# A hybrid layer in fp32 on one core: scales moved from GpSimd to ScalarE, residual sums moved between engines, and new instruction orders

## The chip, the cores and the metric

The kernel runs on one core of a Trainium2 chip. The metric is the device time of one launch in microseconds (us). The engines are TensorE (PE in the profile, with its weight loads as PEld), VectorE (DVE), ScalarE (ACT), GpSimd (POOL) and SyncE (SP).

## What is computed

The input is `x` of 8 batches, 512 tokens and 128 channels, in fp32. Four sub-layers are added to it in turn:

```python
x = x + attn_a(layernorm(x))      # q = n Wq ; (q n^T) n, no softmax
x = x + ffn(layernorm(x))         # f1
x = x + attn_b(layernorm(x))      # RWKV: time mixing, then channel mixing
x = x + ffn(layernorm(x))         # f2, the same weights as f1

# ffn: only expert 0 counts
h = relu(tgt @ w1[0] + b1[0]);  y = tgt + h @ w2[0] + b2[0]
return (y - mean(y)) * rsqrt(var(y) + 1e-5) * gamma + beta

# attn_b
k, v, r = xk @ Wk.T, xv @ Wv.T, xr @ Wr.T       # xk, xv, xr mix a token with the one before
x = x + (sigmoid(r) * wkv(k, v)) @ Wo.T         # wkv: a scan over tokens
kk = square(relu(xk2 @ ffn_Wk.T))
return x + sigmoid(xr2 @ ffn_Wr.T) * (kk @ ffn_Wv.T)
```

Each layer norm and each output of an ffn needs a scale `(var + eps)^-0.5` for each token.

## The kernel before

Each batch is a tile `R[b]` of 128 partitions and 4 rows of 128 tokens (`J = 4`). The residual stream lives in `R[b]` from the first load to the store. The work is cut into small helper functions, one for each batch and step (`attn_gram(b, bank)`, `hidden_up(b, f, n, bank)`, `z_stats(b, f, bank)`), and each engine calls its helpers in an order that is written out by hand, one long list for each engine. So an engine does exactly the next item of its list, and where this item waits on a semaphore, all behind it wait too. Batches are at different sub-layers at the same time, and the eight PSUM banks are dealt out by the numbers in the lists.

The steps that matter here:

- The layer norms: DVE takes the statistics (`row_stats`, `mean_var`), POOL makes the scale in `shift` (an addition of eps), `power` (a power of -0.5) and `bias`, and ACT applies it in `normed`. The first tile is done in two halves (`first_stats`, `first_mean_var`, `first_shift`, `first_power`, `first_normed`, the last one on DVE).
- The attention: PE makes the Gram matrix of the normed tile (`attn_gram`, L1089), the transposes (`transposed`, L1076), the projection (`attn_proj`, L1097) and the product (`attn_apply`, L1104), with an ACT copy out of PSUM after each of the first three. DVE adds the result to `R` (`attn_out`, L535).
- The ffn: transposes of the normed tile, `ffn_evacuate`, four `hidden_up` (L1117) with a `relu` on ACT after each (L907), four `ffn_down` (L1126) that add up in one bank. The sum in this bank begins with the ffn's own input (`y = tgt + ...`). For the batches in `STARTED` DVE writes it there (`ffn_start`, L712). For the others PE does, by four transposes (its own `ffn_start`, L1237). PE's other matmuls of 512 columns are `cmix_up` (L1188) and the three products of the time mixing (L1159, L1164, L1169).
- The ffn's output: `z_stats` and `mean_var` on DVE, then `z_shift` (L341) and `power` (L346) on POOL make `f_zn_rs`, and DVE's `ffn_scaled` (L566) multiplies by it and by gamma. The result is added to `R` in one of two ways: by a DMA with accumulation that POOL starts (`ffn_sum`, L382), or for the batches in `ADDED` by DVE (`ffn_add`, L573). The channel mixing's result has the same two ways: `cmix_sum` (L390, a DMA from POOL) and `cmix_out` (L703, on DVE).
- The last tile is done in two halves: `last_down`, `last_stats`, `last_mean_var`, `last_shift`, `last_power`, `last_scaled`, `last_out`, and a store for each half.

ACT loads one table at its start, `natural_log_exp_and_others`, and no other.

## Time and profile before

| | |
|---|---|
| median of 3 runs | 262.93 us (262.4 to 263.28) |
| the profiled execution: its own time | 264.55 us |
| the profiled execution: span from the first to the last instruction | 262.8 us |
| mean granted TensorE clock | 0.994 |
| PE busy | 253.0 us (96%) |
| DVE busy | 232.7 us (89%) |
| ACT busy | 227.4 us (87%) |
| POOL busy | 153.1 us (58%) |
| DMA | 16.53 MB |

Times in the rows are in microseconds from the start of the span. "Busy" is the union of an engine's instructions. The profiled execution took 1.62 us longer than the median of the runs. PE's instructions are pipelined: a row of one matmul shows more than the distance to the next one.

### The profile page before, as it was taken

The page shows a single profiled execution, that of the slowest core. Times are in us where ns is not written, and L with a number is a line of the kernel's source. Part 1 is how long each engine was busy: PE and PEld are TensorE (multiplying, and loading weights), DVE is VectorE, ACT ScalarE, POOL GpSimd, SP SyncE. Part 2 cuts the span into 40 slices and gives each one's busy share as a digit, 9 for nine tenths or more (in the row PEclk, how much of TensorE's full clock was granted, in tenths as well). Part 3 has the DMA queues.
Part 4 walks back from the last instruction along what each step waited for, and adds up shares of the span by engine and source line. Part 5 has one row for each costly group of instructions (what it writes and reads, how often), then busy time and mean ns, then how long its engine had stood idle before and what let it go on. Part 6 is the DMA issues. An engine that isn't in the chain of part 4 may idle for free.

```text
span 262.8 us, 5291 instructions
## 1 busy us (share of the span) xinstructions
PE 253.0 (96%) x1508; PEld 189.6 (72%) x1508; DVE 232.7 (89%) x762; ACT 227.4 (87%) x439; POOL 153.1 (58%) x290
## 2 busy tenths in 40 slices
PE   7999999999999999999999999999999999999991
PEld 6877686778777686667677767757874977777771
DVE  4598699999999999999999999999999987816384
ACT  1589899988988999899999999999999999993640
POOL 4558788832984774657927166964817158353522
PEclk9999999999999999999999999999999999999997
DMA  7922202402024220222403142063222526450332
GB/s 204 300 90 41 41 2 41 80 0 42 1 44 80 40 40 4 40 41 42 81 1 60 22 80 42 1 115 69 50 49 49 110 46 108 94 114 12 64 96 80
DMA packets 16908, 16.53 MB, mean 63 GB/s; under 512 B 1392, under 2 KB 11504, under 8 KB 16880
## 3 DMA queue, kind: packets, MB, share of 16 engines
q0 software_dynamic: 5616, 10.23, 22.9%
q1 hardware_dynamic: 10848, 5.84, 8.0%
q8 instruction: 12, 0.20, 0.3%
q10 hardware_dynamic: 416, 0.14, 0.2%
q14 instruction: 16, 0.13, 0.2%
HBM read 3.87 MB, written 2.10 MB: 23 GB/s over the span
## 4 chain that ended last, share of the span: by engine, by line
PE 84%; ACT 4%; POOL 4%; issue 3%; DVE 3%; DMA 1%; DVEq 0%; ACTq 0%; POOLq 0%
PE bank L1117 19%; PE bank L1126 19%; PE bank L1188 10%; PE bank L1194 8%; PE bank L1076 7%; PE bank L1089 3%; PE bank L1104 3%; PE bank L1169 3%; PE bank L1164 3%; PE bank L1205 2%; PE bank L1175 2%; PE bank L1159 2%; PE bank L1237 1%; DMA R<-in_hidden 1%; ACT f_h L907 1%
## 5 line engine op out<-in xcount | busy, mean ns | idle before, releaser
L1126 PEld LDWEIGHTS bank<-W,f_h 128*128 128x128 f32 x480 | 59.0, 192 | 12.0 <-issue 11.0
L1117 PE MATMUL bank<-f_yT,W 128*128 128x512 f32 x128 | 63.3, 595 | 0.0
L1126 PE MATMUL bank<-W,f_h 128*128 128x128 f32 x480 | 60.8, 275 | 0.0
L1194 PEld LDWEIGHTS bank<-FWv,KK 128*128 128x128 f32 x256 | 30.9, 192 | 3.4 <-issue 2.6
L1194 PE MATMUL bank<-FWv,KK 128*128 128x128 f32 x256 | 32.2, 276 | 0.0
L1188 PE MATMUL bank<-XK,FWk 128*128 128x512 f32 x64 | 30.5, 596 | 0.8 <-ACT KK L964 0.6
L1117 PEld LDWEIGHTS bank<-f_yT,W 128*128 128x128 f32 x128 | 21.2, 191 | 12.4 <-issue 7.8
L840 ACT ACTIVATE f_y<-R,f_yn_nb,f_yn_rs 128x128 f32<-128x128 f32 x64 | 26.3, 484 | 3.3 <-POOL f_yn_nb L350 3.1
L907 ACT ACTIVATE f_h<-bank,B1C 128x512 f32<-128x512 f32 x36 | 24.3, 686 | 0.2 <-PE bank L1126 0.2
L907 ACT ACTIVATE f_h<-bank,B 128x512 f32<-128x512 f32 x28 | 18.6, 681 | 6.0 <-PE bank L1126 3.3
L293 POOL TENSOR_TENSOR f_yn_ve<-f_yn_mv,K_EPS 128x4 f32<-128x4 f32 x16 | 7.3, 457 | 25.1 <-DVE f_yn_mv L529 25.1
L374 POOL DMA_DIRECT2D R<-BETA x16 | 16.8, 1068 | 6.1 <-ACT f_y L840 5.4
L1188 PEld LDWEIGHTS bank<-XK,FWk 128*128 128x128 f32 x64 | 11.4, 190 | 12.3 <-issue 8.0
L968 ACT ACTIVATE KK<-KK 128x512 f32<-128x512 f32 x32 | 19.6, 633 | 0.2
L341 POOL TENSOR_TENSOR f_zn_ve<-f_zn_mv,K_EPS 128x4 f32<-128x4 f32 x15 | 8.7, 579 | 18.9 <-DVE f_zn_mv L529 18.9
L566 DVE SCALAR_TENSOR_TENSOR f_zg<-bank,f_zn_rs,GAMMA 128x128 f32<-128x128 f32 x56 | 15.6, 339 | 3.5 <-issue 3.3
L964 ACT ACTIVATE KK<-bank 128x512 f32<-128x512 f32 x32 | 18.3, 586 | 0.4 <-PE bank L1188 0.3
L446 DVE BATCH_NORM_STATS2 f_zn_stats<-bank 128x6 f32<-128x128 f32 x60 | 13.2, 280 | 5.6 <-PE bank L1126 5.5
L346 POOL TENSOR_TENSOR f_yn_rs<-f_yn_ve,K_RSQRT 128x4 f32<-128x4 f32 x16 | 16.6, 1037 | 0.0
L346 POOL TENSOR_TENSOR f_zn_rs<-f_zn_ve,K_RSQRT 128x4 f32<-128x4 f32 x15 | 16.1, 1071 | 0.7
L382 POOL DMA_DIRECT2D R<-f_zg x11 | 10.0, 908 | 11.0 <-DVE f_zg L566 10.1
L840 ACT ACTIVATE N<-R,tmix_nb,tmix_rs 128x128 f32<-128x128 f32 x32 | 13.1, 484 | 1.1 <-POOL tmix_nb L350 0.9
(160 smaller groups left out, 637.2 us busy)
## 6 DMA issues: line engine op xcount, KB each, us to landing
R<-BETA POOLq DMA_DIRECT2D x16, 256.0 KB, 3.4
R<-f_zg POOLq DMA_DIRECT2D x11, 256.0 KB, 3.4
R<-N POOLq DMA_DIRECT2D x8, 256.0 KB, 3.7
R<-in_hidden SPq DMA_DIRECT2D x7, 256.0 KB, 5.6
out_x<-R SPq DMA_DIRECT2D x7, 256.0 KB, 2.3
R<-G POOLq DMA_DIRECT2D x4, 256.0 KB, 3.5
W<-in_w SPq DMA_DIRECT2D x2, 256.0 KB, 5.1
BETA<-in_beta SPq DMA_DIRECT2D x1, 256.0 KB, 5.2
```

The lines of the kernel that those rows point to most:

```text
L346: pool.tensor_tensor(n.rs[b % 2][:], n.ve[b % 2][:], K_RSQRT[:], ALU.pow).then_inc(n.scale.sem(b), 1)
L374: pool.dma_start(R[b][:], BETA[:], accum_op=ALU.add).then_inc(*f.xb.step(b))
L566: last = v.scalar_tensor_tensor(zg[:, j, :], z[:, j, :], f.znorm.rs[b % 2][:, j:j + 1], GAMMA[:], ALU.mult, ALU.mult)
L840: done = a.activation(dst[:, j, :], src[:, j, :], ACT.Identity, scale=n.rs[b % 2][:, j:j + 1], bias=n.nb[b % 2][:, j:j + 1])
L907: a.activation(at(f.h, b)[:, n, :], banks[bank][:], ACT.Relu, bias=bias[:, n:n + 1]).then_inc(f.h_ready[n], 1)
L964: a.activation(at(KK, b)[:, n, :], banks[bank][:], ACT.Relu).then_inc(square[n].sem(b), 1)
L968: a.activation(at(KK, b)[:, n, :], at(KK, b)[:, n, :], ACT.Square).then_inc(square[n].sem(b), 1)
L1076: last = t_.matmul(banks[bank][:, j * P:(j + 1) * P], src[:, j, :], IDENT[:], start=(j == 0), stop=(j == J - 1), is_transpose=True, skip_g ...
L1117: t_.matmul(banks[bank][:], W1[:, n * P:(n + 1) * P], at(f.yT, b)[:], start=True, stop=True).then_inc(f.h_psum[n], 1)
L1126: last = t_.matmul(banks[bank][:, j * C:(j + 1) * C], at(f.h, b)[:, n, j * P:(j + 1) * P], W2[:, n, :], start=False, stop=(n == H - 1), sk ...
L1188: t_.matmul(banks[bank][:], FWk[:, n * P:(n + 1) * P], at(XK2, b)[:], start=True, stop=True).then_inc(kk_psum[n], 1)
L1194: last = t_.matmul(banks[bank][:, j * C:(j + 1) * C], at(KK, b)[:, n, j * P:(j + 1) * P], FWv[:, n, :], start=(n == 0 and j == 0), stop=(n ...
```

## The change

Four things change.

1. ACT makes some scales that POOL made before, as `exp(-0.5 * ln(var + eps))` with two activations from the table that is already loaded: for the two halves of the first tile (`first_log`, `first_root`), for all outputs of both ffns (`z_log`, `z_root`) and for the two halves of the last one (`last_log`, `last_root`). That is 19 pairs (2, 15 and 2), 38 activations. `z_shift`, `first_shift`, `last_shift` and the powers that follow them are gone from POOL's list.
2. `ADDED` shrinks from (0, 4), (5, 6, 7), (0, 1, 6, 7) to (0,), (7,), (7,). Three `ffn_add` (f1: 4; f2: 5, 6) and three `cmix_out` (0, 1, 6) leave DVE, and six DMAs with accumulation join POOL's list. `ffn_add` has no call left and is removed.
3. `STARTED` of f2 grows from (5, 6, 7) to (4, 5, 6, 7): one more sum is begun in PSUM by DVE, and one group of four PE transposes goes away. This makes eight such sums.
4. All lists are in a new order, with new bank numbers. Nothing else changes in what is computed.

```diff
-ADDED = {"f1": (0, 4), "f2": (5, 6, 7), "x3": (0, 1, 6, 7)}
+ADDED = {"f1": (0,), "f2": (7,), "x3": (7,)}
-STARTED = {"f1": (0, 1, 2, 3), "f2": (5, 6, 7)}
+STARTED = {"f1": (0, 1, 2, 3), "f2": (4, 5, 6, 7)}
...
-            def ffn_add(b, f, tile):
-
-                dve.wait_ge(f.zg_ready, b + 1)
-                dve.wait_ge(*f.xb.ready(b))
-                v.tensor_tensor(R[b][:], at(tile, b)[:], R[b][:], ALU.add).then_inc(*f.out.step(b))
...
+            def log_rows(n, rows, wait, b, done):
+
+                act.wait_ge(*wait)
+                if b >= 2:
+                    act.wait_ge(f2.zg_ready, b - 1)
+                c = slice(rows[0], rows[-1] + 1)
+                a.activation(n.ve[b % 2][:, c], n.mv[b % 2][:, c, 1], ACT.Ln, bias=K_EPS[:, 0:1]).then_inc(done, 1)
+
+            def root_rows(n, rows, wait, b, done):
+
+                act.wait_ge(*wait)
+                c = slice(rows[0], rows[-1] + 1)
+                a.activation(n.rs[b % 2][:, c], n.ve[b % 2][:, c], ACT.Exp, scale=-0.5).then_inc(done, 1)
...
+            def z_log(b, f):
+                n = f.znorm
+                act.wait_ge(const_ready, 8)
+                act.wait_ge(n.mv_ready, b + 1)
+                if b >= 2:
+                    if b - 2 in f.split:
+                        act.wait_ge(*f.out.ready(b - 2))
+                    else:
+                        act.wait_ge(f.zg_ready, b - 1)
+                a.activation(n.ve[b % 2][:], n.mv[b % 2][:, :, 1], ACT.Ln, bias=K_EPS[:, 0:1]).then_inc(n.scale.sem(b), 1)
+
+            def z_root(b, n):
+
+                act.wait_ge(*n.scale.done(b, "ve"))
+                a.activation(n.rs[b % 2][:], n.ve[b % 2][:], ACT.Exp, scale=-0.5).then_inc(n.scale.sem(b), 1)
...
-            gram_evacuate(0, 0); attn_evacuate(0, 1); proj_evacuate(0, 0); attn_normed(1); attn_normed(2)
+            first_log(0); first_root(0); first_log(1); first_root(1); gram_evacuate(0, 1); attn_evacuate(0, 0)
...
-            attn_gram(0, 0); attn_transpose(0, 1); attn_proj(0, 0); bias_rows(); attn_apply(0, 0)
+            attn_transpose(0, 0); attn_gram(0, 1); attn_proj(0, 1); attn_apply(0, 1); attn_transpose(1, 0)
```

The first place is the start of PE's list. The rows before, from the warm-up matmuls (L1213) on:

```order
1 L1213 MATMUL bank<-WROW 128x128 x10
2 L1089 MATMUL bank<-XN 128x128 x4
3 L1076 MATMUL bank<-IDENT,XN 128x128 x4
4 L1097 MATMUL bank<-GRAM,Wq 128x128
5 L1220 MATMUL bank<-DIAG,MEAN 128x128
6 L1221 MATMUL bank<-VEC,MEAN 128x1
7 L1104 MATMUL bank<-PROJ,XNT 128x128 x4
8 L1076 MATMUL bank<-IDENT,XN 128x128 x4
```

And the same place after the change (L1114 are transposes, L1127 the Gram matrix, L1135 the projection, L1142 the product, L1258 the bias rows):

```order
1 L1251 MATMUL bank<-WROW 128x128 x10
2 L1114 MATMUL bank<-IDENT,XN 128x128 x4
3 L1127 MATMUL bank<-XN 128x128 x4
4 L1135 MATMUL bank<-GRAM,Wq 128x128
5 L1142 MATMUL bank<-PROJ,XNT 128x128 x4
6 L1114 MATMUL bank<-IDENT,XN 128x128 x4
7 L1127 MATMUL bank<-XN 128x128 x4
8 L1114 MATMUL bank<-IDENT,XN 128x128 x4
9 L1135 MATMUL bank<-GRAM,Wq 128x128
10 L1127 MATMUL bank<-XN 128x128 x4
11 L1258 MATMUL bank<-DIAG,MEAN 128x128
```

The first tile's transposes now stand ahead of its Gram matrix, and the bias rows, which stood between the projection and the product, stand behind the third Gram matrix. On ACT, further down, the transposes' copy `attn_evacuate(3)` and `attn_normed(3)` also stand earlier, so that PE has the transposes and the Gram matrix of the fourth tile ahead of the first `hidden_up`.

The second place is in the middle of ACT's list, around the exponents of the time mixing's third tile. Before (L927 to L940 are the four passes over the exponents, L885 and L896 copies out of PSUM, L964 a relu):

```order
88 L927 ACTIVATE EB<-EA 128x1024
89 L896 ACTIVATE f_yT<-bank,B2C 128x512
90 L885 ACTIVATE PROJ<-bank 128x128
91 L932 ACTIVATE EA<-EA 128x2x512
92 L936 ACTIVATE EB<-EB 128x1024
93 L940 ACTIVATE EA<-EA 128x2x512
94 L964 ACTIVATE KK<-bank 128x512
```

After (the same passes are L915, L920, L924 and L928; L1012 is `z_log`, L1017 `z_root`):

```order
101 L915 ACTIVATE EB<-EA 128x1024
102 L861 ACTIVATE XNT<-bank 128x512
103 L884 ACTIVATE f_yT<-bank,B2C 128x512
104 L924 ACTIVATE EB<-EB 128x1024
105 L873 ACTIVATE PROJ<-bank 128x128
106 L1012 ACTIVATE f_zn_ve<-f_zn_mv,K_EPS 128x4
107 L920 ACTIVATE EA<-EA 128x2x512
108 L934 ACTIVATE G<-bank 128x512
109 L928 ACTIVATE EA<-EA 128x2x512
110 L1017 ACTIVATE f_zn_rs<-f_zn_ve 128x4
```

The scale of an ffn output has joined the line, its logarithm and its exponential apart, with three other activations between them.

The third place is in DVE's list, at the ffn output of the fifth tile of f1. Before (L566 scales it, L573 adds it to `R`; L648 is a sum of the time mixing):

```order
130 L566 SCALAR_TENSOR_TENSOR f_zg<-bank,f_zn_rs,GAMMA 128x128 x4
131 L624 TENSOR_TENSOR EA<-EA,bank 128x512
132 L643 TENSOR_TENSOR AB<-AB,EB 128x2x512
133 L579 TENSOR_TENSOR DX<-XA 128x512
134 L573 TENSOR_TENSOR R<-f_zg,R 128x512
135 L648 TENSOR_TENSOR EA<-AB,EA 128x1024
```

After (the scaling is L560, and the sum of the time mixing L636):

```order
128 L560 SCALAR_TENSOR_TENSOR f_zg<-bank,f_zn_rs,GAMMA 128x128 x4
129 L523 BN_AGGR f_yn_mv<-f_yn_stats 128x2 x4
130 L607 TENSOR_TENSOR EV<-EB,bank 128x512
131 L612 TENSOR_TENSOR EA<-EA,bank 128x512
132 L677 SCALAR_TENSOR_TENSOR DC<-DC,VEC,XC 128x512
133 L567 TENSOR_TENSOR DX<-XA 128x512
```

The addition is gone from DVE; POOL starts a DMA for it instead. In the same way `cmix_out(0)` and `cmix_out(1)` are gone further down.

## Rows read from the trace of the kernel before

**Rows 1.** The page's busy line: us (share of the span) xinstructions.

```profile
PE 253.0 (96%) x1508; PEld 189.6 (72%) x1508; DVE 232.7 (89%) x762; ACT 227.4 (87%) x439; POOL 153.1 (58%) x290
```

**Rows 2.** PE's groups by shape: names, shapes xcount | busy us, mean ns.

```profile
L1117 PE MATMUL bank<-f_yT,W 128*128 128x512 f32 x128 | 63.3, 595 | 0.0
...
L1188 PE MATMUL bank<-XK,FWk 128*128 128x512 f32 x64 | 30.5, 596 | 0.8 <-ACT KK L964 0.6 <-ACT f_h L907 0.2
...
L1159 PE MATMUL bank<-XK,Wk 128*128 128x512 f32 x16 | 8.3, 600 | 0.0
...
L1237 PE MATMUL bank<-IDENT,f_yT 128*128 128x128 f32 x36 | 5.5, 276 | 0.0
```

**Rows 3.** The chain of work that ended last: start us, us, what.

```profile
18.95 3.44 PE bank L1117 x8
23.28 2.68 PE bank L1126 x24
```

**Rows 4.** The timeline of the first 20 us: start us, us, engine, instructions [idle before].

```profile
1.46 4.64 PE L1213 MATMUL bank<-WROW 128*128 128x128 f32 x20 [1.46 <-DVE WROW L723]
...
4.56 0.25 DVE L457 BATCH_NORM_AGGREGATE attn_mv<-attn_stats 128x2 f32<-128x6 f32 x2
...
6.40 0.60 DVE L471 TENSOR_SCALAR XN<-R,attn_mv,attn_rs 128x128 f32<-128x128 f32 x2 [0.33 <-POOL attn_rs L308]
...
7.15 2.04 PE L1089 MATMUL bank<-XN 128*128 128x128 f32 x8 [1.05 <-DVE XN L471]
...
8.99 1.06 PE L1076 MATMUL bank<-IDENT,XN 128*128 128x128 f32 x4
9.23 0.28 ACT L879 ACTIVATE GRAM<-bank 128x128 f32<-128x128 f32 x1 [6.17 <-PE bank L1089]
...
9.84 0.63 PE L1097 MATMUL bank<-GRAM,Wq 128*128 128x128 f32 x2
...
10.58 0.27 ACT L885 ACTIVATE PROJ<-bank 128x128 f32<-128x128 f32 x1
...
10.73 3.18 ACT L840 ACTIVATE XN<-R,attn_nb,attn_rs 128x128 f32<-128x128 f32 x8
...
15.87 1.65 ACT L840 ACTIVATE f_y<-R,f_yn_nb,f_yn_rs 128x128 f32<-128x128 f32 x4
...
18.79 3.60 PE L1117 MATMUL bank<-f_yT,W 128*128 128x512 f32 x8
```

**Rows 5.** Stretches: us, busy us (xcount) of PE, PEld, DVE, ACT, POOL, clock, DMA.

```profile
7.00:20.00 13.00, 12.44 (x77) 10.93 (x78) 9.95 (x62) 9.54 (x27) 7.10 (x17) 1.00 0.70 192
...
80.00:220.00 140.00, 138.66 (x804) 100.18 (x804) 138.51 (x396) 136.53 (x251) 82.26 (x140) 1.00 0.29 51
...
220.00:240.00 20.00, 20.00 (x134) 16.03 (x133) 11.81 (x40) 18.49 (x37) 8.88 (x16) 1.00 0.48 93
```

**Rows 6.** ACT's smallest activations, whole span.

```profile
L993 ACT ACTIVATE WDEC<-WEXP 128x1 f32<-128x1 f32 x1 | 0.2, 203 | 0.0
L991 ACT ACTIVATE WEXP<-VEC 128x1 f32<-128x1 f32 x1 | 0.2, 194 | 0.0
```

**Rows 7.** DVE's additions to R that leave it, between 40 and 200 us.

```profile
L703 DVE TENSOR_TENSOR R<-G,R 128x512 f32<-128x512 f32 x2 | 1.4, 675 | 0.0
L573 DVE TENSOR_TENSOR R<-f_zg,R 128x512 f32<-128x512 f32 x1 | 0.7, 676 | 0.0
```

**Rows 8.** POOL's shifts of the ffn outputs, between 80 and 220 us.

```profile
L341 POOL TENSOR_TENSOR f_zn_ve<-f_zn_mv,K_EPS 128x4 f32<-128x4 f32 x7 | 5.1, 727 | 5.9 <-DVE f_zn_mv L529 5.9
```

**Rows 9.** The DMA issues: count, KB each, median us to landing.

```profile
R<-G POOLq DMA_DIRECT2D x4, 256.0 KB, 3.5
```

**Rows 10.** The timeline of the end.

```profile
255.32 1.95 PE L1146 MATMUL bank<-W,f_h 128*128 128x128 f32 x16
...
256.42 0.49 DVE L451 BATCH_NORM_STATS2 f_zn_stats<-bank 128x6 f32<-128x128 f32 x2 [0.29 <-PE bank L1146]
...
258.71 1.18 DVE L497 SCALAR_TENSOR_TENSOR R<-f_zg,f_zn_rs,R 128x128 f32<-128x128 f32 x4
```

More of the change, by code:

```diff
@@ L826, in _ @@
[L826 to L828 removed]
+            warm_tile(); first_stats(0); first_mean_var(0); first_stats(1); first_mean_var(1); first_normed(0)
+            first_normed(1); attn_stats(1); mean_var(1, na); attn_stats(2); mean_var(2, na); attn_stats(3)
@@ new lines, in _ @@
+            ffn_out(0, f1); tmix_stats(0); mean_var(0, nt); attn_out(3, 2); decay_along_tokens(); ffn_stats(3, f1)
+            attn_stats(7); mean_var(3, f1.norm); mean_var(7, na); ffn_start(2, f1, 4, (f1.h_ready[3], 2))
+            z_stats(1, f1, 0); mean_var(1, f1.znorm); tmix_change(0); mix_k(0); ffn_scaled(1, f1, 0); mix_v(0)
+            mix_r(0); running_max(0, 1); differences(0, 1); ffn_start(3, f1, 5); attn_out(4, 2); tmix_stats(1)
+            mean_var(1, nt); ffn_stats(4, f1); mean_var(4, f1.norm); z_stats(2, f1, 4); new_values(0, 6)
@@ new lines, in _ @@
+            denominator_sum(0); numerator_sum(0); first_values(0, 6); weighted(0); mean_var(2, f1.znorm)
+            with_current(0); tmix_change(1); gate_sum(0); mix_k(1); ffn_scaled(2, f1, 4); gate_log(0, 1)
+            running_max(1, 3); gated(0); mix_v(1); differences(1, 3); attn_out(5, 6); tmix_out(0, 0); ffn_stats(5, f1)
+            mix_r(1); mean_var(5, f1.norm); up_bias(7); tmix_stats(2); first_values(1, 1); mean_var(2, nt)
+            cmix_stats(0); new_values(1, 1); mean_var(0, ncm); z_stats(3, f1, 5); denominator_sum(1); numerator_sum(1)
@@ new lines, in _ @@
+            attn_out(6, 6); weighted(1); mean_var(3, f1.znorm); ffn_stats(6, f1); with_current(1)
+            mean_var(6, f1.norm); tmix_change(2); gate_sum(1); mix_k(2); ffn_scaled(3, f1, 5); gate_log(1, 0)
+            running_max(2, 1); mix_v(2); gated(1); mix_r(2); differences(2, 1); z_stats(4, f1, 3); tmix_stats(3)
+            mean_var(4, f1.znorm); mean_var(3, nt); cmix_change(0); tmix_out(1, 6); cmix_k(0); cmix_stats(1)
+            attn_out(7, 6); mean_var(1, ncm); ffn_stats(7, f1); ffn_scaled(4, f1, 3); mean_var(7, f1.norm)
@@ new lines, in _ @@
+            z_stats(6, f1, 7); weighted(3); tmix_change(4); with_current(3); ffn_stats(0, f2); gate_sum(3)
+            mean_var(0, f2.norm); mix_k(4); mix_v(4); gate_log(3, 1); ffn_scaled(5, f1, 5); running_max(4, 2)
+            gated(3); cgate_log(1, 6); differences(4, 2); cmix_change(2); mean_var(6, f1.znorm); tmix_stats(5)
+            cmix_gated(1, 4); cmix_k(2); mean_var(5, nt); tmix_out(3, 5); mix_r(4); ffn_scaled(6, f1, 7)
+            cmix_stats(3); denominator_sum(4); cmix_r(2); new_values(4, 3); mean_var(3, ncm); first_values(4, 3)
@@ new lines, in _ @@
+            mean_var(2, f2.norm); first_values(5, 4); weighted(5); tmix_change(6); with_current(5); mix_k(6)
+            gate_sum(5); cmix_change(4); cmix_k(4); tmix_stats(7); gate_log(5, 1); mean_var(7, nt); running_max(6, 3)
+            gated(5); cgate_log(3, 4); mix_v(6); cmix_r(4); differences(6, 3); cmix_gated(3, 0); mix_r(6)
+            z_stats(0, f2, 5); mean_var(0, f2.znorm); tmix_out(5, 0); cmix_stats(5); mean_var(5, ncm)
+            ffn_scaled(0, f2, 5); tmix_change(7); ffn_stats(3, f2); mix_k(7); new_values(6, 0); mean_var(3, f2.norm)
@@ L831, in _ @@
+            last_mean_var(1); last_scaled(1, 1); last_out(0); last_out(1)
         @block.scalar
```

487 lines of the change are left out of this document (233 added, 254 removed).

## The prediction

> **What bounds the kernel now.** I read the page's busy line first [rows 1]: PE is busy for 96% of the span, DVE for 89%, ACT for 87%, POOL for 58%. A busy PE is not yet a PE at its peak, since the ends of its instructions are modelled. So I turned to the pace. In the chain of work, 24 matmuls of 128 columns take 2.68 us and 8 of 512 columns 3.44 us [rows 3], that is 0.112 and 0.43 us each. The groups by shape give the counts [rows 2]: 128 and 64 of 512 columns, and three groups of 16 like the one shown, 240 in all. The page has 1508 matmuls [rows 1], of which 20 are the warm-up [rows 4], so 1248 are narrow. The work is 240 x 0.43 + 1248 x 0.112 = 242.6 us. PE does it between 7.15 us, when the first Gram matrix starts, and 257.27 us, when the last matmul ends (255.32 + 1.95) [rows 4, 10]. That is 250.1 us, so 7.5 us are lost in between. Of these, 3.3 us fall before 20 us: 77 matmuls start there, the last three of them wide, worth 9.6 us, in the 12.85 us from 7.15 on [rows 5]. Only 4.2 us are left for the other 237 us. PE is the bound nearly everywhere, and a gain can come from four places: less work on PE, an earlier start, a shorter end, and the 4.2 us.
>
> The stretches say what stands right behind PE [rows 5]. Between 80 and 220 us DVE is idle for 1.49 of 140 us and ACT for 3.47. Both are nearly full, and an engine that gets more work there can take over as the bound.
>
> **The change part by part.** *One sum more begun in PSUM by DVE.* PE has 36 transposes for it in nine groups of four [rows 2] and loses one group: 4 x 0.112 = 0.45 us off the bound. DVE writes 512 columns more, 0.68 us by an addition of this size [rows 7]; by its tile it lies between 220 and 240 us, where DVE was idle for 8.2 us [rows 5]. Without this cover it would cost 0.68.
>
> *The first tile's scale on ACT.* The statistics of its second half are done at 4.81 us (4.56 + 0.25), the normed half begins at 6.40 after a wait for POOL, and ends at 7.00 [rows 4]. ACT needs two activations. The nearest rows are two of one column, 0.19 and 0.20 us [rows 6]; a bound from above is the copy of 128 columns, 0.28 us [rows 4]. I take 0.2 each, 0.4 for a pair, since four columns are nearer to one than to 128. With it the second half can be normed from about 5.4 to 6.05 us (DVE has the first half from 4.85). PE's warm-up ends at 6.10 [rows 4], so PE loses its 1.05 us of idle time there and starts real work at about 6.05, 1.1 us earlier.
>
> It doesn't keep all of it. The transposes now go first, 0.85 us (four at 0.21, from 1.06 us with the modelled end), so that the Gram matrix starts at 6.9 and its copy at 8.95 + 0.05, against 9.23. Then the projection needn't wait for the transposes until 9.84: it starts at 9.3 and its copy at 10.0, against 10.58. So `attn_normed(1)` and the two behind it are some 0.6 us earlier (from 10.73, 3.18 us for two tiles) [rows 4], and end at about 13.3. From there I add up ACT's list in its new order, with durations from the rows: a Gram copy 0.27, two copies of 512 columns 1.06 in the old run's pace (0.53 each), a projection copy 0.27, `attn_normed(3)` 1.6, a Gram copy 0.27, the ffn's first normed tile 1.65. The sum is 5.1, so this tile ends at 18.4, against 17.52. In the old run the first `hidden_up` starts 1.27 us behind that end [rows 4]; now it would be at 19.7 with this distance, and at 19.3 if ACT's instructions overlap as in the old run (eight activations of a normed tile take 3.18 us, though each takes 0.48 by itself). I take 19.3: half a microsecond later than the old 18.79. But by then PE has done the transposes and the Gram matrix of the fourth tile as well, 4 + 8 = 12 matmuls or 1.34 us, which stood behind it before. Net: 1.34 - 0.5 = 0.85 us. The bounds are 0.45 (start at 19.7) and 1.3 (no delay at all).
>
> *The end.* `last_scaled(0)` moves into the wait between the statistics and their mean. The rest of the chain is DVE's own: from 256.42 to 259.89 (258.71 + 1.18) it does 3.3 us of work, and POOL's scale isn't what it waits for [rows 10]. ACT's faster scale gives nothing here, the new order perhaps 0.15 us; bounds 0 and 0.3.
>
> *The ffn outputs' scales on ACT.* In the stretch from 80 to 220 us POOL made seven of them [rows 8]. Seven pairs at 0.4 are 2.8 us, less than ACT's 3.47 us of idle time, so I cost them at nothing; the cover is thin. With 0.28 for an activation it would be 3.9 us, 0.45 over. Behind each logarithm stand copies and relus that PE waits for, and it waits itself for DVE's `mean_var`.
>
> The Trainium skill says in "ScalarE: Activation LUTs", "Rules for kernel authors", that a tight latency budget should count about 0.3 us for each ACTIVATE and 0.83 ns for each element. By this rule a pair would cost about 0.61 us, seven pairs 4.3 us, ACT would be 0.8 us over, and the sum would give 262.3 us. The rows of one column show 0.19 and 0.20 us, so the trace does not agree; it has no row of this form with four columns.
>
> *Six sums to POOL's DMAs.* Three of them leave DVE between 80 and 200 us, 3 x 0.68 = 2.0 us [rows 7], more than DVE's idle time there. The result lands 3.5 us after the issue [rows 9], 2.8 later than by DVE. The tile is next read by `tmix_stats` or `ffn_stats`, and the lists hold other batches' work ahead of those. POOL gives up 19 scales for six DMAs, and is idle for 57.7 of 140 us [rows 5] before. I cost it at nothing, with the relief of DVE as a possible gain inside the 4.2 us.
>
> *New orders in the middle.* I can't add up 237 us of four lists from rows. The loss there was 4.2 us, and this bounds the gain. I take no change: DVE has 2.0 us less, ACT 2.8 us more, and both were near full.
>
> The sum is 0.45 + 0.85 + 0.15 = 1.45 us. The profiled execution goes from 264.55 to 263.1; its own time is 1.62 us above the median of the runs shown, and I take the same step off the median: 262.93 - 1.45 = 261.5 us.
>
> **The rivals.** *A, the forecast:* 261.5 us, by itself between 260.6 and 262.3. Chance 0.47.
>
> *B, the middle tightens.* DVE's three additions are gone, its queue runs ahead, and half of the 4.2 us goes: 261.5 - 2.1 = 259.4 us. For it: DVE was idle for only 1% between 80 and 220 us. Against: ACT gets the work instead. A second source would be the pace at the start. The eight matmuls at 7.15 take 2.04 us, 0.21 apart where the granted clock's column has 1.00 [rows 4, 5]; that is the pace of 1.2 GHz, half of that of [rows 3], after PE had been idle for 1.05 us. Without this idle time the change to the fast pace may come sooner, which would shorten the transposes and the Gram matrix by up to 1.2 us. Chance 0.17.
>
> *C, ACT becomes the bound (slower).* The place is `z_log` in ACT's list. POOL waited 5.9 us for DVE's `mean_var` ahead of these seven scales [rows 8], at no cost, since nothing urgent stood behind it. On ACT the relus for PE stand behind. If ACT waited as long, it would be 2.8 + 5.9 - 3.5 = 5.2 us over, and the time 266.7. With 60% of the wait, 3.5 us, it is 2.8 over: 264.3 us, my figure for this case. It is slower by more than the measurement can tell from 2.2 us over on, that is from 2.9 us of waits. For it: DVE is as full as ACT and its delay would pass on directly. Against: in the second place of the order `z_log` stands five activations behind the exponents' first pass, while DVE has the statistics and mean right behind the differences that this pass waits for; a list of this kind may keep the waits short. Chance 0.20.
>
> *D, the start gives nothing.* PE starts earlier but the chain of copies, `attn_normed(3)` above all, holds the first `hidden_up` back until 20.1 us, and the 12 matmuls done ahead only make up for it. Then 0.45 + 0.15 are left, 262.3 us, and with a microsecond lost on a new wait 263.3. Chance 0.16.
>
> **How the numbers follow.** About 0.3% of 262.93 us, 0.79 us, is what a measurement of this kernel can tell from no change: the bounds are 262.14 and 263.72. Faster: nine tenths of A and all of B, 0.42 + 0.17, and a little of D, 0.61 in all. Slower: C and a rest of D, 0.20. Same: 0.19. The likeliest is A, 261.5. The range takes in B's 259.4 with its own spread down to 259.0 and C's 264.3 at the other end; below 259.0 and above 264.3 I leave 0.1 each.
>
> **What would show it.** In the new profile: the first transpose at about 6.05 us and no idle time behind the warm-up; the first `hidden_up` at 19.3; 32 transposes of the group that had 36; activations of four columns of about 0.2 us; ACT's idle time between 80 and 220 us near 0.7, and no wait of ACT for `f_zn_mv` above a microsecond in sum; the work of PE 0.45 us less and its loss after 20 us still about 4.2. The prediction is wrong if that loss is above 6 (C) or below 2.5 (B), or if the logarithms wait for DVE.

## The result, and the profile after

The changed kernel takes 259.39 us (median of 4 runs, 259.09 to 259.62), and the kernel before on the same chip 262.95 us (262.4 to 263.28). The ratio is 0.9845 with a 95% interval of 0.9803 to 0.9887. The gain is 3.6 us, where 1.45 was predicted. The new time lies inside the range of 259.0 to 264.3 us, on rival B's figure of 259.4.

Executions of the kernel before come near 262.9, 264.3 and 265.8 us, and the one shown ahead of the prediction took 264.55. So I profiled the same kernel again (`b_again`, profiled execution 263.11 us, span 261.3), and compare with that where a microsecond matters. The profiled execution of the changed kernel took 259.21 us, with a span of 257.4.

From the page of the changed kernel and its groups by shape: the busy line, the shares of the chain that ended last (PE had 84% of it before), the group of wide matmuls for `FWk`, and the DMA issues of the sums (KB each, median us to landing).

```profile
PE 249.5 (97%) x1504; PEld 187.8 (73%) x1504; DVE 231.2 (90%) x757; ACT 231.9 (90%) x477; POOL 133.2 (52%) x258
...
PE 94%; DVE 2%; DMA 1%; ACT 1%; POOL 1%; issue 0%; DVEq 0%; POOLq 0%; ACTq 0%
...
L1226 PE MATMUL bank<-XK,FWk 128*128 128x512 f32 x64 | 32.0, 597 | 0.0
...
R<-G POOLq DMA_DIRECT2D x7, 256.0 KB, 3.4
...
R<-f_zg POOLq DMA_DIRECT2D x14, 256.0 KB, 4.0
```

PE has four matmuls fewer, which are the four transposes. In [rows 2] the `FWk` group had 0.8 us of idle time ahead of its members. Now it has none.

The stretches of the changed kernel, with the columns of [rows 5]:

```profile
7.00:20.00 13.00, 11.84 (x86) 10.02 (x86) 11.61 (x70) 10.87 (x30) 7.77 (x22) 1.00 0.69 192
...
80.00:220.00 140.00, 139.97 (x831) 102.88 (x831) 136.06 (x387) 138.66 (x268) 72.76 (x128) 1.00 0.30 53
100.00:200.00 100.00, 100.00 (x588) 72.92 (x587) 99.59 (x279) 99.46 (x192) 50.83 (x90) 1.00 0.29 51
...
220.00:240.00 20.00, 20.00 (x120) 14.83 (x119) 14.52 (x57) 15.79 (x36) 5.54 (x11) 1.00 0.45 87
```

And the same hundred microseconds of the kernel before, in its second profile:

```profile
100.00:200.00 100.00, 98.70 (x567) 70.53 (x566) 99.61 (x273) 97.80 (x179) 60.39 (x100) 1.00 0.26 46
```

PE's column is the one to read. Between 80 and 220 us it goes from 138.66 to 139.97 of 140 us, and between 100 and 200 us it is now full. ACT goes from 136.53 to 138.66, which leaves it 1.34 us of idle time. The view of PE's waits names neither ACT nor another engine after the first 20 us. In the kernel before it named ACT three times, for 0.6, 0.4 and 0.2 us, and VectorE never. These are the first two, from the second profile (us in all, times, longest):

```profile
PE bank L1188 <- ACT KK L964: 0.6, 1, 0.6
PE bank L1076 <- ACT f_h L907: 0.4, 1, 0.4
```

Each of the two stands behind an activation of ACT that had waited in its turn for a product of POOL (`tmix_nb` and `cmix_nb`, the biases of two norms). So the old kernel's losses run through ACT and POOL as well as through VectorE.

Modelled ends hide part of a wait, so I counted the loss as the prediction did: from the start of each matmul to that of the next, less its own 0.112 or 0.43 us [rows 3]. Counted to the start of the last matmul, the 4.2 us of the prediction are 4.0.

| | first profile before | second profile before | after |
|---|---|---|---|
| first real matmul starts | 7.15 | 7.03 | 5.88 |
| lost from there to 20 us | 3.38 | 2.04 | 2.66 |
| lost from 20 to 100 us | 0.80 | 0.79 | 0.42 |
| lost from 100 to 200 us | 2.71 | 2.70 | 0.71 |
| lost from 200 us to the last matmul | 0.51 | 0.51 | 0.23 |
| span | 262.8 | 261.3 | 257.4 |

The two profiles of the kernel before differ at the head alone. After 20 us they lose the same time.

Of 3.9 us of span, 2.0 come from the middle, 0.45 from the transposes, some 0.5 from the start (1.15 earlier, 0.6 more lost), 0.4 and 0.3 from the stretches on both sides of the middle. What is left, some 0.25 us, is the end. From the last tile's first statistics to the last sum's end the new timeline has 254.41 - 251.32 = 3.1 us, where [rows 10] has 3.5; behind it comes the last store, which ends 2.9 to 3.3 us later in five profiles of the changed kernel and its small edits.

The timeline of the changed kernel's head, and of its end:

```profile
1.46 4.63 PE L1251 MATMUL bank<-WROW 128*128 128x128 f32 x20 [1.46 <-DVE WROW L711]
...
4.35 0.29 ACT L982 ACTIVATE attn_ve<-attn_mv,K_EPS 128x2 f32<-128x2 f32 x1 [1.29 <-DVE attn_mv L451]
...
4.68 0.20 ACT L988 ACTIVATE attn_rs<-attn_ve 128x2 f32<-128x2 f32 x1
...
5.88 0.98 PE L1114 MATMUL bank<-IDENT,XN 128*128 128x128 f32 x4
...
6.70 1.06 PE L1127 MATMUL bank<-XN 128*128 128x128 f32 x8
...
9.17 3.19 ACT L828 ACTIVATE XN<-R,attn_nb,attn_rs 128x128 f32<-128x128 f32 x8 [0.18 <-POOL attn_nb L350]
...
18.15 3.60 PE L1155 MATMUL bank<-f_yT,W 128*128 128x512 f32 x8
...
251.32 0.49 DVE L445 BATCH_NORM_STATS2 f_zn_stats<-bank 128x6 f32<-128x128 f32 x2 [2.60 <-PE bank L1184]
...
253.28 1.13 DVE L491 SCALAR_TENSOR_TENSOR R<-f_zg,f_zn_rs,R 128x128 f32<-128x128 f32 x4
```

PE no longer waits behind the warm-up. The Gram matrix's eight matmuls take 1.06 us from 6.70 on, where [rows 4] has 2.04 from 7.15 on. `attn_normed(1)` begins at 9.17 instead of 10.73.

ACT's new instructions, by their lines (duration ns least/median/greatest, first and last start; and below each, what it waited for in us, times):

```profile
L1012 ACT ACTIVATE f_zn_ve<-f_zn_mv,K_EPS x15: 280/294/315, 27.3 to 247.0; 128x4 f32<-128x4 f32 x15
...
  DVE f_zn_mv L523: 1.7, 2
...
L1017 ACT ACTIVATE f_zn_rs<-f_zn_ve x15: 191/198/217, 27.6 to 247.3; 128x4 f32<-128x4 f32 x15
...
  DVE f_zg L560: 1.0, 1
```

A pair is 0.49 us, not 0.4. ACT waits 1.7 us for `f_zn_mv` in the whole span, in two places, and not at all between 80 and 220 us, where POOL had waited 5.9 [rows 8].

### The profile page after: what moved, and what is told of

Its sections match the earlier page's. It is cut to its first block, busy times and chain, and to the rows that moved or that the text cites. A ratio compares the mean times of both kernels' runs of the same rounds, so it can differ in the third digit from the quotient of the medians.

```text
span 257.4 us, 5284 instructions
## 1 busy us (share of the span) xinstructions
PE 249.5 (97%) x1504; PEld 187.8 (73%) x1504; DVE 231.2 (90%) x757; ACT 231.9 (90%) x477; POOL 133.2 (52%) x258
## 4 chain that ended last, share of the span: by engine, by line
PE 94%; DVE 2%; DMA 1%; ACT 1%; POOL 1%; issue 0%; DVEq 0%; POOLq 0%; ACTq 0%
PE bank L1155 21%; PE bank L1164 21%; PE bank L1232 11%; PE bank L1226 11%; PE bank L1114 7%; PE bank L1213 3%; PE bank L1243 3%; PE bank L1197 3%; PE bank L1207 3%; PE bank L1202 3%; PE bank L1142 3%; PE bank L1127 2%; PE bank L1275 1%; DMA R<-in_hidden 1%; PE bank L1175 1%; PE bank L1135 1%
## 5 line engine op out<-in xcount | busy, mean ns | idle before, releaser
L1164 PEld LDWEIGHTS bank<-W,f_h 128*128 128x128 f32 x480 | 58.2, 192 | 8.7 <-issue 8.6
L1155 PE MATMUL bank<-f_yT,W 128*128 128x512 f32 x128 | 61.2, 593 | 0.0
L1226 PE MATMUL bank<-XK,FWk 128*128 128x512 f32 x64 | 32.0, 597 | 0.0
L895 ACT ACTIVATE f_h<-bank,B 128x512 f32<-128x512 f32 x32 | 21.2, 681 | 5.5 <-PE bank L1155 4.2
L390 POOL DMA_DIRECT2D R<-G x7 | 6.3, 897 | 36.4 <-DVE G L686 36.4
L895 ACT ACTIVATE f_h<-bank,B1C 128x512 f32<-128x512 f32 x32 | 21.4, 682 | 0.1
L382 POOL DMA_DIRECT2D R<-f_zg x14 | 14.1, 1006 | 13.4 <-DVE f_zg L560 11.2
L346 POOL TENSOR_TENSOR f_yn_rs<-f_yn_ve,K_RSQRT 128x4 f32<-128x4 f32 x16 | 19.3, 1206 | 0.0
L560 DVE SCALAR_TENSOR_TENSOR f_zg<-bank,f_zn_rs,GAMMA 128x128 f32<-128x128 f32 x56 | 15.6, 338 | 3.2 <-issue 2.2
L374 POOL DMA_DIRECT2D R<-BETA x16 | 15.7, 1037 | 4.6 <-ACT f_y L828 4.0
L1226 PEld LDWEIGHTS bank<-XK,FWk 128*128 128x128 f32 x64 | 10.7, 190 | 8.2 <-issue 4.4
L440 DVE BATCH_NORM_STATS2 f_yn_stats<-R 128x6 f32<-128x128 f32 x64 | 13.7, 275 | 0.1
```

The source lines that it names most:

```text
L346: pool.tensor_tensor(n.rs[b % 2][:], n.ve[b % 2][:], K_RSQRT[:], ALU.pow).then_inc(n.scale.sem(b), 1)
L374: pool.dma_start(R[b][:], BETA[:], accum_op=ALU.add).then_inc(*f.xb.step(b))
L440: last = v.bn_stats(n.stats[b % 2][:, j, :], src[:, j, :])
L895: a.activation(at(f.h, b)[:, n, :], banks[bank][:], ACT.Relu, bias=bias[:, n:n + 1]).then_inc(f.h_ready[n], 1)
L1155: t_.matmul(banks[bank][:], W1[:, n * P:(n + 1) * P], at(f.yT, b)[:], start=True, stop=True).then_inc(f.h_psum[n], 1)
L1164: last = t_.matmul(banks[bank][:, j * C:(j + 1) * C], at(f.h, b)[:, n, j * P:(j + 1) * P], W2[:, n, :], start=False, stop=(n == H - 1), sk ...
```

## The experiments

Each ran beside the kernel before on the same chip. The ratio is to that kernel, with its 95% interval. It takes in that kernel's long executions, so it can show more gain than the differences in microseconds, which are to the medians 262.95 and 259.39. In the names `a_` is the changed kernel with an edit, `b_` the kernel before with one. Of long lists, only the first lines that tell the edit are shown.

**b_again, a_again: the two kernels as they are.**

> The kernel before, unchanged, profiled once more. Its first profiled execution had a time of 264.55 us, 1.6 above its median. Theory 1 (the 1.6 us are waits of that one execution, most of them among the 4.2 us that PE lost after 20 us): the new profile has a time near 262.9 and PE loses 2.5 to 3 us after 20 us. Theory 2 (the profile was typical and the median of the runs is of another kind): the same 4.2 us are lost, at the same places, 110.6 and 125.0 us above all. Ratio 1.000 within 0.003 under both.

> The changed kernel, unchanged, beside the others of this set. Both theories: within 0.4 us of 259.4. In the profile PE loses less than 1 us between 100 and 200 us, as in the first one.

The kernel before gave 262.99 us (0.9982, 0.9946 to 1.0017) and the changed one 258.96 (0.9823, 0.9782 to 0.9863). So differences below some 0.5 us between two edits aren't read as anything. `b_again` decides neither of its theories whole: the time came back to the median, as the first said, but the 4.0 us lost after 20 us stayed, as the second said. What the first profile had more of was lost ahead of 20 us.

**a_addvec: three sums back on VectorE, in the new orders.**

```diff
-ADDED = {"f1": (0,), "f2": (7,), "x3": (7,)}
+ADDED = {"f1": (0, 4), "f2": (7,), "x3": (0, 1, 7)}
...
+            new_values(2, 2); first_values(2, 2); ffn_add(4, f1, f1.zg); cmix_r(0); tmix_change(3); numerator_sum(2)
...
+            cmix_gated(0, 4); cmix_out(0); mean_var(5, f1.znorm); denominator_sum(3); mean_var(2, ncm)
...
+            mean_var(6, f1.znorm); tmix_stats(5); cmix_gated(1, 4); cmix_out(1); cmix_k(2); mean_var(5, nt)
```

> The changed kernel with three of the six sums back on VectorE, the ones in the full middle (the ffn output of the fifth tile of f1, the channel mixing of the first two tiles), 2.0 us of work between 80 and 200 us. Theory 1 (VectorE is the engine that held PE up in the middle, and its relief is what took the 4.2 us away): 1.5 to 2 us slower, 260.9 to 261.4, and PE loses time again between 90 and 200 us. Rival (the new orders hide it): less than 0.5 us slower, below 259.9.

261.34 us (0.9882, 0.9841 to 0.9923), 2.0 us above the changed kernel (2.4 above `a_again`): as much as three additions of 0.68 us [rows 7], or a little more. PE's loss between 100 and 200 us is back at 2.69 us. The view of PE's waits says for what it waited (us in all, times, longest); the changed kernel has neither row:

```profile
PE bank L1282 <- DVE EA L618: 0.5, 1, 0.5
...
PE bank L1233 <- DVE N L664: 0.2, 1, 0.2
```

PE waits for VectorE itself. In the new orders VectorE is what stands behind PE in the middle, and three additions less on it are 2 us less. The two rows hold 0.7 of the 2.0 us; the rest is spread over gaps too short for this view. In the old orders PE's waits named ACT, so this run doesn't say what the additions cost there. The next one does.

**b_addtiny: the same relief in the old orders.** The three additions stay where they are, but work on one column of each 128; 127 of 128 columns of these three sums are left out.

```diff
-                v.tensor_tensor(R[b][:], at(tile, b)[:], R[b][:], ALU.add).then_inc(*f.out.step(b))
+                c = 1 if f is f1 else C
+                v.tensor_tensor(R[b][:, :, 0:c], at(tile, b)[:, :, 0:c], R[b][:, :, 0:c], ALU.add).then_inc(*f.out.step(b))
```

> The kernel before, old orders, in which VectorE does three of its additions to R (the ffn output of f1's fifth tile, the channel mixing of the first two) on one column of each row in place of all 128: it leaves out 127 of 128 columns of these sums, and gets 1.8 us of relief between 95 and 125 us without any transfer to wait for. Theory 1 (VectorE is what held PE up between 100 and 200 us in the kernel before too): PE's loss there falls from 2.7 to about 0.9, time 261.0 to 261.4. Rival (in the old order PE waits for single items, not for VectorE's work as a whole): less than 0.7 us faster, above 262.2.

262.05 us (0.9939, 0.9914 to 0.9964): 0.9 us gained (1.2 against the median beside it, 263.21), between the two theories. PE's loss between 100 and 200 us goes from 2.70 to 1.79 us. One stall is gone, that of 0.61 us ahead of `FWk` for `KK` [rows 2 has it as "ACT KK L964 0.6"]. The wait of 0.4 us for `f_h` is still there. The relief alone is worth about half of what it is worth in the new orders. It did one thing more: none of its 12 executions took over 262.5 us, where 10 of 23 of the kernel before beside them took over 264. Why is not shown.

**b_addpool: the sums really moved, in the old orders.**

```diff
-ADDED = {"f1": (0, 4), "f2": (5, 6, 7), "x3": (0, 1, 6, 7)}
+ADDED = {"f1": (0,), "f2": (5, 6, 7), "x3": (6, 7)}
...
+            back_shift(3); bias(7, f1.norm); ffn_sum(4, f1, f1.zg); shift_twice(4); power(4, nt); back_power(3)
...
-            tmix_change(3); ffn_add(4, f1, f1.zg); with_current(2); z_stats(5, f1, 6); tmix_stats(4); mix_k(3)
```

> The kernel before with three of its additions to R in the middle (one ffn output, two of the channel mixing) moved from VectorE to DMAs that GpSimd starts; all orders and all scales as before. Theory 1 (VectorE held PE up in the middle, whatever the order): the 2.7 us that PE loses between 100 and 200 us shrink by 1.5 to 2, time 261.0 to 261.5. Theory 2 (the relief is worth something only together with the new orders, which place other work in the gap): less than 0.5 us faster, above 262.4.

268.4 us (1.0176, 1.0134 to 1.0219), 5.4 us slower, where both theories had it faster or the same. In its profiled execution (269.45 us), VectorE's waits in the timeline:

```profile
100.00 0.87 DVE L447 BATCH_NORM_STATS2 tmix_stats<-R 128x6 f32<-128x128 f32 x4 [2.81 <-DMA R<-f_zg]
...
117.32 0.87 DVE L447 BATCH_NORM_STATS2 f_yn_stats<-R 128x6 f32<-128x128 f32 x4 [1.29 <-DMA R<-G]
```

In the old list `tmix_stats(4)` stood three items behind the addition that it needs, and now waits 2.81 us for the landing. Only part of this is the transfer. `f_zg` was done at 92.9 us, but POOL issued the DMA at 96.70, behind an addition of four columns that took 2.24 us:

```profile
94.22 2.24 POOL L356 TENSOR_TENSOR tmix_ve<-tmix_mv,K_EPS 128x4 f32<-128x4 f32 x1
...
96.70 0.86 POOL L382 DMA_DIRECT2D R<-f_zg  x1
```

So the place in POOL's list, which I chose, is in this price as well. The whole list behind it is late, and PE loses 9.1 us between 100 and 200 us. The prediction said that "the lists hold other batches' work ahead of those". The new lists do; the old ones didn't.

**b_moves: every move of the change, none of its new orders.** It has the new `ADDED` and `STARTED` and all scales on ACT; what is moved is put into the old lists at the nearest place.

```diff
-ADDED = {"f1": (0, 4), "f2": (5, 6, 7), "x3": (0, 1, 6, 7)}
+ADDED = {"f1": (0,), "f2": (7,), "x3": (7,)}
...
-STARTED = {"f1": (0, 1, 2, 3), "f2": (5, 6, 7)}
+STARTED = {"f1": (0, 1, 2, 3), "f2": (4, 5, 6, 7)}
```

> The kernel before with all moves between engines of the change (19 scales to ScalarE, six sums to DMAs, one sum more begun in PSUM by VectorE), each put in at the nearest place of the old lists; old orders otherwise. Theory 1 (the moves make the gain, the orders only carry them): 259.5 to 260.7. Theory 2 (the new orders make it): 262 to 264, so that 2.5 us and more are left to the orders.

286.32 us (1.085, 1.0804 to 1.0896): 23 us slower. With the new orders the same moves gain 3.6 us. My places may not be the best that the old lists allow, so the 23 us are the price of these places. The run shows that the moves don't bring the gain wherever they are put; that no place in the old lists would have brought it is not shown.

**b_zact: the ffn outputs' scales on ACT, in the old orders.**

```diff
-            ffn_residual(1, f1); shift(5, na); power(5, na); bias(2, f1.norm); shift(6, na); z_shift(0, f1)
-            power(0, f1.znorm); power(6, na); bias(5, na); shift_twice(0); bias(6, na); power(0, nt); bias(0, nt)
...
+            attn_normed(5); z_log(0, f1); z_root(0, f1.znorm); tmix_normed(0); ffn_evacuate(2, f1, 2)
```

> The kernel before with the scales of the fifteen ffn outputs made on ScalarE (logarithm and exponential put into ScalarE's list ahead of the first item whose input VectorE finishes later), all else as before. Theory 1 (the scale's engine is worth little by itself: it was hidden on GpSimd): 262.4 to 263.5. Theory 2 (the short scale is the gain): faster than 262. Theory 3 (ScalarE becomes the bound in the old order, by 15 pairs of 0.5 us and their waits): 264 to 267.

278.84 us (1.057, 1.0516 to 1.0625), 16 us slower, in the direction of the third theory and much further. Most of it is lost before 100 us. VectorE's waits in that kernel say why:

```profile
DVE f_zg L561 <- ACT f_zn_rs L1024: 7.0, 4, 3.2
...
DVE R L547 <- ACT f_zn_rs L1024: 5.8, 1, 5.8
```

The pair stands behind too much of ACT's list, and VectorE waits for it: 12.8 us in these five places, where fifteen pairs are 7.4 us of work. Most of the price is that of the place, which was mine again, and not of the 0.49 us.

**a_zpool, a_zpoolmid: the same scales back on POOL, in the new orders.** The first puts all fifteen back, the second six of them (f1's batches 4 to 7, f2's 0 and 1), in POOL's list in the order in which VectorE finishes what they need.

```diff
-            shift_twice(0); power(0, nt); bias(0, nt); back_shift(0); bias(5, na); ffn_residual(2, f1); back_power(0)
+            z_shift(0, f1); power(0, f1.znorm); shift_twice(0); power(0, nt); bias(0, nt); back_shift(0); bias(5, na)
...
-            ffn_evacuate(1, f1, 2); decay_rates(); z_log(0, f1); z_root(0, f1.znorm); proj_evacuate(3, 4)
-            relu(1, f1, 0, 2); relu(1, f1, 1, 1); ffn_normed(2, f1); relu(1, f1, 2, 7); relu(1, f1, 3, 4)
...
+            ffn_evacuate(1, f1, 2); decay_rates(); proj_evacuate(3, 4); relu(1, f1, 0, 2); relu(1, f1, 1, 1)
```

> The changed kernel with the scales of the fifteen ffn outputs made on POOL again (a shift and a power, put into POOL's list in the order in which VectorE finishes their inputs); the first and the last tile's scales stay on ScalarE. Theory 1 (the scales were hidden on POOL and are hidden on ScalarE, the new orders tighten the middle): within 0.5 us of the changed kernel, 259.0 to 260.0. Rival (the shorter way of the scale, 0.4 us in place of 1.6 and of POOL's queue, is what lets VectorE run ahead and PE lose nothing): 1.5 to 3 us slower, 261 to 262.5, with waits of VectorE for the scale.

> The changed kernel with the scales of six ffn outputs in the full middle (f1's last four, f2's first two) made on POOL again; the other nine stay on ScalarE. ScalarE has 3 us less there. Theory 1 (POOL's longer way, 1.3 us and its queue, is what the new orders have no room for): 260 to 263, with waits of VectorE for the scale, and less than the 8 us of all fifteen. Rival (only the early tiles need the short scale, and ScalarE was nearly the bound in the middle): 258.5 to 259.2.

267.51 us (1.0089, 1.0052 to 1.0126) for all, 261.91 us (0.9941, 0.9912 to 0.9971) for six: 8.1 and 2.5 us over the changed kernel. With all, VectorE waits for POOL's scale; in the changed kernel it waits less, for ACT's. The rows of `a_zpool` and of the changed kernel, over the whole span:

```profile
DVE f_zg L566 <- POOL f_zn_rs L346: 4.5, 3, 2.2
```

```profile
DVE f_zg L560 <- ACT f_zn_rs L1017: 1.0, 1, 1.0
```

Only 0.7 of the 4.5 us lie between 80 and 220 us. More than half of what PE loses in `a_zpool` after 20 us (7.9 us, against 1.4 in the changed kernel) is lost ahead of 100 us. A pair is over 1.2 us on POOL (below) and 0.49 on ACT; that the new orders live on this difference is argued from these waits. The places in POOL's list are mine, too. The stretches of the second kernel, whose profiled execution was a long one (263.78 us against its median of 261.91):

```profile
80.00:220.00 140.00, 137.34 (x791) 98.59 (x791) 135.02 (x382) 133.51 (x247) 81.59 (x134) 1.00 0.29 52
```

ACT is busy for 5.2 us less than in the changed kernel, and PE, which it was to relieve, for 2.6 us less. The largest stall in it isn't a late `f_zn_rs`. PE waits 1.1 us for a relu behind ACT's `NC`, and ACT waited 2.6 us there for this product of four columns:

```profile
115.51 2.52 POOL L350 TENSOR_TENSOR cmix_nb<-cmix_nm,cmix_rs 128x4 f32<-128x4 f32 x1
```

VectorE's wait for POOL's scale is 0.7 us in all. "ACT's work at no cost" was right; that POOL's was at no cost in the new orders was my theory, and it fell. In POOL's list one of the added pairs (112.18 to 113.53 us) stands right ahead of the work for `cmix_nb`, so it makes this later too.

**a_started567: the sum of f2's fifth tile begun by PE again, in the new orders.**

```diff
-STARTED = {"f1": (0, 1, 2, 3), "f2": (4, 5, 6, 7)}
+STARTED = {"f1": (0, 1, 2, 3), "f2": (5, 6, 7)}
...
-            ffn_down(4, f2, 0, 2); cmix_down(6, 0, 7, (f2.h_ready[2], 5)); ffn_down(4, f2, 1, 2)
+            ffn_start(4, f2, 2, (f2.h_ready[0], 5)); ffn_down(4, f2, 0, 2); cmix_down(6, 0, 7, (f2.h_ready[2], 5))
```

> The changed kernel with the sum of the fifth tile of f2 begun by PE's four transposes again, as before the change. Theory 1 (PE is the bound of the changed kernel, so its work counts in full): 0.45 us slower than the changed kernel, about 259.6. Rival (there is room at that place): no difference, 259.1.

259.84 us (0.9854, 0.9829 to 0.9879): 0.45 above the changed kernel's first median and 0.9 above its second. The first is no more than the noise, so the time alone doesn't show the term. The profile bears it out: PE has the four matmuls more and loses 1.3 us after 20 us, as in the changed kernel (1.4), so nothing hides them.

**a_firstpool: the first tile's scale back on POOL, in the new orders.**

```diff
-            shift(1, na); power(1, na); bias(1, na); shift(2, na); power(2, na); bias(2, na); shift(3, na)
+            first_shift(0); first_power(0); first_shift(1); first_power(1); shift(1, na); power(1, na); bias(1, na)
```

> The changed kernel with the first tile's two scales made on POOL again, all else as changed. Theory 1 (the start gives about 2 us: 1.2 from the scale on ScalarE, which also takes the idle time away ahead of the first matmul and lets the fast pace begin sooner): 1.2 to 2.0 us slower than the changed kernel, 260.6 to 261.4, and the Gram matrix of the first tile takes 2.0 us again in place of 1.06. Rival (the start is worth the 0.85 us of the prediction, the middle the rest): 0.5 to 0.9 us slower, 259.9 to 260.3.

260.0 us (0.9829, 0.9792 to 0.9866): 0.6 to 1.0 us above the changed kernel, less than my theory's 1.2 to 2, and in the rival's range. The first transpose starts at 5.96 us all the same, since it needs the first half of the tile alone. The scale's share shows behind it. The Gram matrix starts at 7.30 instead of 6.70, and its eight matmuls take 1.09 us, not the 2.0 of my theory.

**b_firstact: the same scale on ACT, in the old orders.**

```diff
-            first_shift(0); first_power(0); first_shift(1); first_power(1); shift(1, na); power(1, na); bias(1, na)
...
+            first_log(0); first_root(0); first_log(1); first_root(1); gram_evacuate(0, 0); attn_evacuate(0, 1)
```

> The kernel before with only the first tile's two scales made on ScalarE; all orders as before. Theory 1 (the start's chain gets 0.6 us shorter and the idle time ahead of the first Gram matrix shorter too): the fastest runs 0.4 to 0.7 us faster, 262.2 to 262.5, and fewer runs at 264.3 and above, since the pause in which the slow pace survives is shorter. Rival (the chain of the second and third tile holds the start anyway): no difference, and the same levels.

264.25 us (1.0015, 0.9978 to 1.0052): no gain. In its profiled execution (264.13 us) the first `hidden_up` starts at 16.74 us instead of 17.34, 0.6 us earlier, and PE loses 1.5 us more between 140 and 160 us. POOL's and VectorE's timelines there, of `b_firstact` and then of `b_again`:

```profile
139.89 2.30 POOL L350 TENSOR_TENSOR cmix_nb<-cmix_nm,cmix_rs 128x4 f32<-128x4 f32 x1
...
140.92 1.20 DVE L647 TENSOR_TENSOR EA<-AB,EA 128x1024 f32<-128x1024 f32 x1
```

```profile
139.76 1.21 DVE L643 TENSOR_TENSOR AB<-AB,EB 128x1024 f32<-128x1024 f32 x1
...
140.47 0.56 POOL L350 TENSOR_TENSOR cmix_nb<-cmix_nm,cmix_rs 128x4 f32<-128x4 f32 x1
```

One product of four columns took 1.7 us longer, and ACT waited for it:

```profile
ACT NC L839 <- POOL cmix_nb L350: 1.4, 1, 1.4
```

So in this execution what the start gave was taken back a hundred microseconds later by an operation that the edit hasn't touched. In both kernels it ends 0.06 to 0.07 us behind the end of an addition or product of VectorE (142.12 and 140.97 us), in `b_firstact` two instructions of VectorE later. This doesn't explain all: the shortest executions of `b_firstact`, 262.95 to 263.01 us, aren't below those of the kernel before either.

**a_gramfirst, b_warm12: what the head's pace hangs on.** The first lets the Gram matrix go ahead of the transposes again. The second makes the old warm-up 24 matmuls long, to fill PE's idle time of 1.05 us [rows 4].

```diff
-            attn_transpose(0, 0); attn_gram(0, 1); attn_proj(0, 1); attn_apply(0, 1); attn_transpose(1, 0)
+            attn_gram(0, 1); attn_transpose(0, 0); attn_proj(0, 1); attn_apply(0, 1); attn_transpose(1, 0)
```

```diff
-            warm_up(0, 10)
+            warm_up(0, 12)
```

> The changed kernel with the first tile's Gram matrix ahead of its transposes again (PE's order before). The chain of copies that follows hangs on the Gram matrix. Theory 1 (the start is bound by this chain, and the transposes fill PE's wait for the first copy): 0.3 to 0.5 us faster than the changed kernel, 258.5 to 258.7. Rival (the transposes fit in while the second half is normed, so that nothing is lost by them): no difference or slower, since the Gram matrix has to wait for both halves.

> The kernel before with twelve warm-up matmuls in place of ten, so that PE's idle time of 1.05 us ahead of the first Gram matrix is nearly gone; all else as before. Theory (the idle time decides in which runs the fast pace of 0.112 us comes before the first Gram matrix and in which only after 10 us): the runs no longer spread over 262.8, 264.3 and 265.8, they all lie within a microsecond. Rival (the levels have another cause): the same three levels.

259.35 us (0.9834, 0.9809 to 0.9858) and 262.9 us (0.9977, 0.9952 to 1.0003). Neither is told apart from its base. In the profile of `a_gramfirst` the first matmul starts at 6.06 us. So either alone, the new order (`a_firstpool`, 5.96) or ACT's scale (here), brings PE's first matmul close behind its warm-up. With the longer warm-up, which leaves 0.3 us of that idle time in its profile, 2 of 12 executions took over 264 us, against 9 of 23 of the kernel before beside them. These are too few to say that long executions became rarer, and they didn't end, as my theory wanted. That the idle time delays the fast pace is at most part of the reason for them.

## Why the prediction was off, point by point

- **PE is the bound nearly everywhere, DVE and ACT right behind it: right, with POOL left out.** POOL was taken as half idle, but its scales and the products behind them stand behind ACT's waits in the kernel before, in `a_zpoolmid` and in `b_firstact`.
- **One more sum begun in PSUM, 0.45: right as far as the runs can tell.** `a_started567` costs 0.45 to 0.9 us, and its profile has the four matmuls in full.
- **The start, 0.85: right in part, too large.** The first transpose came at 5.88 (said: 6.05), and the first `hidden_up` at 18.15 (19.3). Against the second profile of before the start is 1.15 us earlier with 0.6 us more lost, so some 0.5 us are kept; putting the scale back cost 0.6 to 1.0. The prediction laid the idle time of 1.05 us to POOL's scale alone. In `a_firstpool`, with POOL's scale and the new order, the first transpose starts at 5.96 us, so the order alone takes it away as well. I measured the start against a profile in which the slow pace of the first matmuls had lasted until 10.7 us. In `b_again` it had not, and its first `hidden_up` started at 17.34 instead of 18.79. The gain of the start is not the same in each execution, and I gave it as one number.
- **The end, 0.15: 0.4 on VectorE, some 0.25 in the span.** For VectorE's own part the bound of 0.3 was too low: it does the same work there with fewer gaps, 3.1 us in each profile with the new orders that I measured. What comes behind it varies by as much.
- **The ffn outputs' scales, 0: right as a cost, wrong as a view of them.** ACT took the work within its idle time, as [rows 5] allowed, and rival C didn't come: 1.7 us of waits, where 2.9 would have decided. They are still above the microsecond that I named as the most to be seen. But I costed the removal from POOL at nothing as well, since POOL was idle for 57.7 of 140 us. With the new orders POOL's making them costs 8.1 us for all and 2.5 for six, at the places that I gave them. An engine that is half idle can still be the one that is waited for.
- **My 0.2 us for an activation of four columns was off by half for one of the two.** The logarithm takes 0.294 us, above the 0.28 taken as the bound, and the exponential 0.198. The Trainium skill's figure in "ScalarE: Activation LUTs", "Rules for kernel authors", is about 0.3 us for an ACTIVATE that reads its bias from an operand. The trace agrees with it for the logarithm, whose bias is the column `K_EPS`. The exponential has an immediate scale and no such column, so this figure isn't about it; the prediction had left the condition out. The pair stands between the two sums, 0.49 us instead of 0.4 or 0.61. It changed nothing, since ACT kept 1.34 us of idle time.
- **The middle at nothing is the step that failed: "Six sums to POOL's DMAs", costed "at nothing", and "New orders in the middle. I take no change".** With the scales, which were at nothing too, they were worth 2.0 us between 100 and 200 us and 0.7 around it. The prediction had the right number at hand, "DVE has 2.0 us less", and DVE idle for 1% beside PE, and set ACT's 2.8 us more against it. The two don't cancel. In the new orders VectorE's three additions cost 2.0 us (`a_addvec`), while ACT's pairs stand where they hold up nothing that PE waits for. How the 2.0 us divide between sums and orders depends on which is changed first: in the old orders the same relief is worth 0.9 us (`b_addtiny`), since PE's other waits there ran through ACT. The sign to look for, a loss after 20 us below 2.5, came: 0.42 + 0.71 + 0.23 = 1.4 us. Rival B was the right one, and for its main reason. Its figure of 259.4 is luck in part: it has 2.1 us from the middle and 0.85 from the start, where 2.7 and 0.5 were measured. Its second source, a sooner fast pace, shows at the head (1.06 instead of 2.04 us), but only against the first profile of before.
- **Not seen: how much the moves hang on the places in the lists.** I judged a sum's landing by the new lists. In the old ones, at the places that I gave them, the same moves cost 5.4 us (three sums), 16 (the scales) and 23 (all).

What stays open: how much of the 0.7 us between 20 and 100 us and after 200 us belongs to which part, and why executions of the kernel before differ by up to 3 us. Between the two profiles of the kernel before, the pace at the head is nearly the whole difference. In `b_firstact` it was one long operation of POOL. That these are all isn't shown. Open, too, is how much a better place for the moved items would have saved in the old lists, and in POOL's new one.

## What to carry to other kernels

When three engines are over 97% busy in a stretch, don't set work taken off one against work put on another. Here three additions of 0.68 us on VectorE were worth 2.0 us where PE's waits named VectorE, and 0.9 where they named ACT, while 38 activations more on ACT cost nothing that shows. Ask which engine the bound's waits name, and what that engine waited for itself. A change that moves work from one hand-ordered list to another is to be costed with its new order, never as a sum of moves: the distance from the producer to the first reader has to cover the new latency. And take two profiles of the kernel before, so as not to count its own spread as a gain.
